# Decoder layer on one core: cross attention with the values as the stationary operand, weights normalised ahead of their transposes, and no transposes of the output

## The reference

```python
q = (query @ Wq.T).reshape(batch, seq, 16, 64)     # 16 heads of 64
k = (key   @ Wk.T).reshape(batch, seq, 16, 64)
v = (value @ Wv.T).reshape(batch, seq, 16, 64)
weights = jnp.einsum('bqhd,bkhd->bhqk', q, k) * scale + reweight + causal
weights = jax.nn.softmax(weights, axis=-1)
out = jnp.einsum('bhqk,bkhd->bqhd', weights, v).reshape(batch, seq, -1)
return out @ Wo.T + bo
```

## Time and profile before

| | |
|---|---|
| median of 3 runs | 1305.52 us (1304.98 to 1308.28) |
| the profiled execution | 1298.92 us, of it span 1297.2 us |
| PE busy | 1187.7 us, 92% |
| PEld busy | 988.4 us, 76% |
| DVE busy | 830.5 us, 64% |
| ACT busy | 648.9 us, 50% |
| POOL busy | 153.4 us, 12% |
| mean granted clock of TensorE | 0.944 |

### The profile page before, as it was taken

How to read it: one execution, slowest core, us unless ns; L and a number is a source line. 1 busy time by engine, 2 the same in 40 slices (tenths; PEclk the granted TensorE clock), 3 DMA queues, 4 the chain that set the end, 5 groups by cost and what they waited for, 6 DMA issues and landing times.

```text
span 1297.2 us, 22848 instructions
## 1 busy us (share of the span) xinstructions
PE 1187.7 (92%) x8404; PEld 988.4 (76%) x8404; DVE 830.5 (64%) x2630; ACT 648.9 (50%) x1363; POOL 153.4 (12%) x184
## 2 busy tenths in 40 slices
PE   3899899889889989979999988989999999999996
PEld 3767788766788877769876778877778787788875
DVE  5725437873646874645776445778778677788563
ACT  2236533235634224744233643438666776968663
POOL 4899302200000000000000000000000000000000
PEclk9999979999979999998999987989998899999898
DMA  8200000100000010000010200120000010000000
GB/s 313 85 17 1 1 1 1 49 17 1 2 1 1 1 53 14 2 1 1 1 34 17 68 1 1 41 82 25 1 1 25 1 33 25 1 18 26 26 17 17
DMA packets 21388, 33.27 MB, mean 26 GB/s; under 512 B 11424, under 2 KB 12192, under 8 KB 20128
## 3 DMA queue, kind: packets, MB, share of 16 engines
q1 hardware_dynamic: 21280, 31.82, 7.3%
HBM read 27.62 MB, written 4.19 MB: 25 GB/s over the span
## 4 chain that ended last, share of the span: by engine, by line
PE 74%; DVE 13%; ACT 8%; issue 3%; POOL 1%; DVEq 0%; ACTq 0%; POOLq 0%
PE ps L504 41%; PE ps L747 6%; PE ps L645 4%; PE ps L663 2%; PE ps L662 2%; DVE z L1589 2%; DVE arena L1779 2%; PE ps L661 2%; DVE arena L1406 2%; PE ps L637 1%; PE ps L635 1%; PE ps L608 1%; ACT L1263 1%; PE ps L621 1%; PE ps L886 1%
## 5 line engine op out<-in xcount | busy, mean ns | idle before, releaser
L504 PE MATMUL ps<-arena,wts 128*128 128x256 f16 (+1 forms) x1344 | 189.2, 295 | 20.6 <-ACTq L477 20.6
L504 PE MATMUL ps<-wts,arena 128*128 128x256 f32 (+2 forms) x1008 | 201.0, 357 | 3.8 <-ACT arena L1347 3.2
L504 PEld LDWEIGHTS ps<-arena,wts 128*128 128x128 f16 (+1 forms) x1344 | 153.2, 115 | 49.1 <-issue 20.5
L504 PEld LDWEIGHTS ps<-wts,arena 128*128 128x128 f32 (+1 forms) x1008 | 154.6, 155 | 41.3 <-ACT arena L1347 4.0
L1589 DVE SCALAR_TENSOR_TENSOR z<-ps,small,z 128x256 f32<-128x256 f32 x256 | 123.9, 484 | 41.3 <-PE ps L747 26.8
L1197 ACT ACTIVATE pq<-ps 128x512 f32<-128x512 f32 x72 | 43.0, 598 | 169.1 <-PE ps L504 169.0
L747 PE MATMUL ps<-wts,pq 128*128 128x256 f32 x512 | 120.8, 380 | 6.2 <-DVE z L1589 6.2
L747 PEld LDWEIGHTS ps<-wts,pq 128*128 128x128 f32 x512 | 92.6, 190 | 18.7 <-DVE z L1589 4.9
L645 PE MATMUL ps<-ident,pq 128*128 128x128 f32 x384 | 73.9, 306 | 33.1 <-DVE arena L1506 12.3
L1106 ACT ACTIVATE pq<-pq,nms 128x128 f32<-128x128 f32 x128 | 50.9, 398 | 92.1 <-DVE nms L1479 92.1
L1477 DVE CUSTOM_DVE_ANT_0 pq<-ps,mb 128x128 f32<-128x128 f32 x128 | 36.6, 286 | 86.0 <-PE ps L637 85.7
(11 more groups left out here) (286 smaller groups left out, 2402.3 us busy)
## 6 DMA issues: line engine op xcount, KB each, us to landing
cT<-in_cT SPq DMA_DIRECT2D x16, 256.0 KB, 2.7
wts<-in_up SPq DMA_DIRECT2D x1, 2304.0 KB, 15.5
wts<-in_down SPq DMA_DIRECT2D x1, 2304.0 KB, 20.5
xT<-in_xT SPq DMA_DIRECT2D x8, 256.0 KB, 4.0
xin<-in_x SPq DMA_DIRECT2D x8, 256.0 KB, 2.9
xmid<-xin SPq DMA_DIRECT2D x8, 256.0 KB, 2.0
wts<-in_w SPq DMA_DIRECT2D x2, 1024.0 KB, 5.0
wts<-in_c SPq DMA_DIRECT2D x16, 128.0 KB, 3.2
```

The lines of the kernel that those rows point to most:

```text
L504: ins = mm(out_, l, r, start=(n == 0), stop=(n == len(pairs) - 1))
```

## The change

- **Values.** The stationary operand is now the 64 value channels of a head (`V[:, ... AD]`, the column of ones isn't used), and the transposed weights stream: 256 columns for the first half of the keys, 128 for the second. Both heads of a pair go in one iteration (odd `n`), to partitions 0 to 63 and 64 to 127. The output then has channels on partitions, as the output projection wants it; four heads fill a bank (`("OT", s, m)`).
- **Sums.** They are taken by the exps themselves (`accum_out` to `rsum(n)`). DVE takes the reciprocals (`attn_sums`, head n-1).
- **Division.** GpSimd multiplies the weights by them, in place, in front of the transposes (`attn_norm`, mark `Pn`). It does so for every head of every turn; in turn 0 between the expert chunks and those for K, V and Q.
- **Gone:** `turn_out` with its 32 transposes per turn, and DVE's division by sums.
- **Offsets.** Transposes of head n-4 in place of n-3, values of heads n-7 and n-6 in place of n-5, copies out (`turned`, `turned_low`) of head n-7 for both sequences inside the loop. Output projection of sequence 0 in iteration 24 (was 26), of sequence 1 with the first pair of experts (was with the second), transposes of z2 in iteration 28 (was 29).
- **Scratch.** `half` lies at the end of `arena[1]` and no longer on `z2[1]`. The wait for `halfq` and `halfo` above stays as it was.

```diff
+        def rsum(n):
+            return small[1][:, 128 + 2 * (n % 8):130 + 2 * (n % 8)]
...
-        half = flat(z2[1][:, :, :]).bitcast(F16).rearrange("p (i n e) -> p i n e", i=2, n=4)
+        half = arena[1][:, 11 * KC * T:12 * KC * T].bitcast(F16).rearrange("p (i n e) -> p i n e", i=2, n=4)
...
             def attn_turn(n, s, h):
 
-                eng.wait_ge(*pe.at("E", s, h))
+                eng.wait_ge(*pe.at("Pn", s, h))
...
             def attn_values(n, s, h):
 
+
+                if h % 2 == 0:
+                    return
                 V = carve_a(s)[0][2]
-                eng.wait_ge(*pe.at("PT", s, h, "out"))
                 eng.wait_ge(*pe.at("V", s, "out"))
...
-                mm(o[:, c0:c0 + AD + 1], pt[:, 0:P], v0, start=True, stop=True)
-                mm(o[:, c1:c1 + AD + 1], pt[:, P:T], v0, start=True, stop=False)
-                ins = mm(o[:, c1:c1 + AD + 1], pt[:, T:SBLK], v1, start=False, stop=True)
+                m = h // 2
+                if m % 2 == 0:
+                    take(("OT", s, m), ("OT", s, m, "out"), 6 + (n // 4) % 2)
+                o, c = ps[:, 6 + (n // 4) % 2, :], (m % 2) * T
+                for j in range(2):
+                    eng.wait_ge(*pe.at("PT", s, h - 1 + j, "out"))
+                for j in range(2):
+                    hj, row, pt = h - 1 + j, slice(AD * j, AD * j + AD), ptbuf(n - 1 + j)
+                    v0 = V[:, hj * (AD + 1):hj * (AD + 1) + AD]
+                    v1 = V[:, (AH + hj) * (AD + 1):(AH + hj) * (AD + 1) + AD]
+                    mm(o[row, c:c + T], v0, pt[:, 0:T], start=True, stop=False)
+                    ins = mm(o[row, c + P:c + T], v1, pt[:, T:SBLK], start=False, stop=True)
...
-                for n in range(len(UNITS) + 5):
+                for n in range(len(UNITS) + 6):
                     if n < len(UNITS) and n % 2 == 0:
                         attn_scores(n, UNITS[n][0], UNITS[n][1] // 2)
-                    if 0 <= n - 3 < len(UNITS):
-                        attn_turn(n - 3, *UNITS[n - 3])
-                    if 0 <= n - 5 < len(UNITS):
-                        attn_values(n - 5, *UNITS[n - 5])
-
-                    if OUT0 <= n < OUT0 + AM // 2:
-                        turn_out(0, 2 * (n - OUT0), 4 + n % 2)
-                    if n == OUT0 + AM // 2:
+                    if 0 <= n - 4 < len(UNITS):
+                        attn_turn(n - 4, *UNITS[n - 4])
+                    if 0 <= n - 6 < len(UNITS):
+                        attn_values(n - 6, *UNITS[n - 6])
+
+                    if n == OUT0 + 2:
                         out_proj(0, 4 + n % 2)
-                    if n == OUT0 + 7:
+                    if n == OUT0 + 6:
                         transposes(0, "zT2", z2[0], ("z2", 0), 4 + n % 2)
...
-                A(pb[:, 0:P], pb[:, 0:P], ACT.Exp, scale=-1.0, bias=nm[:, 0:1]).then_inc(*act.up())
-                A(pb[:, P:SBLK], pb[:, P:SBLK], ACT.Exp, scale=-1.0, bias=nm[:, 1:2]).then_inc(
+                rs = rsum(n)
+                A(pb[:, 0:P], pb[:, 0:P], ACT.Exp, scale=-1.0, bias=nm[:, 0:1], accum_out=rs[:, 0:1]).then_inc(*act.up())
+                A(pb[:, P:SBLK], pb[:, P:SBLK], ACT.Exp, scale=-1.0, bias=nm[:, 1:2], accum_out=rs[:, 1:2]).then_inc(
                     *act.up(("E", s, h)))
...
+            def attn_sums(n, s, h):
+                eng.wait_ge(*v.at("E", s, h))
+                V_.reciprocal(rsum(n), rsum(n)).then_inc(*v.up(("R", s, h)))
...
                     if n < len(UNITS):
                         attn_max(n, *UNITS[n])
-                    if 0 <= n - 3 < len(UNITS):
-                        attn_pt(n - 3, *UNITS[n - 3])
-                    if 0 <= n - 6 < len(UNITS):
-                        attn_norm(n - 6, *UNITS[n - 6])
...
+                    if 0 <= n - 1 < len(UNITS):
+                        attn_sums(n - 1, *UNITS[n - 1])
+                    if 0 <= n - 4 < len(UNITS):
+                        attn_pt(n - 4, *UNITS[n - 4])
+                    if 0 <= n - 7 < len(UNITS):
+                        turned_low(n - 7, *UNITS[n - 7])
+                    if n == OUT0 + 3:
                         residual(0, "xo", z[0][:, :, :], z2[0], "ln_2")
...
+            def attn_norm():
+                for n, (s, h) in enumerate(UNITS):
+                    pb, rs = pbuf(n), rsum(n)
+                    eng.wait_ge(*po.at("R", s, h))
+                    G.tensor_scalar(pb[:, 0:P], pb[:, 0:P], rs[:, 0:1], None, ALU.mult).then_inc(*po.up())
+                    G.tensor_scalar(pb[:, P:SBLK], pb[:, P:SBLK], rs[:, 1:2], None, ALU.mult).then_inc(
+                        *po.up(("Pn", s, h)))
+
             po.stage("halves")
...
+                if mark == "halfk":
+                    po.turn = 0
+                    attn_norm()
+                    po.turn = None
                 if read:
...
+            po.stage("norms")
+            for g in range(1, TURNS):
+                po.turn = g
+                attn_norm()
+            po.turn = None
```

More of the change, by code:

```diff
@@ L817, in _ @@
                             if e == 0:
-                                for m in range(0, AM, 2):
-                                    turn_out(1, m)
-                            if e == 2:
                                 out_proj(1)
@@ L1199, in _ @@
                         if s == 0:
-                            if e == 0:
-                                for m in range(0, AM, 2):
-                                    turned(1, m)
                             if e == 4:
@@ L1507, in lower, with turned_low @@
                                  parts[:, 0].rearrange("p k t -> p (k t)"), ALU.subtract).then_inc(*v.up(outmark))
-            def turned_low(s, m):
-                if v.turn:
+            def turned_low(n, s, h):
+                m = h // 2 - 1
+                if v.turn and h % 4 == 3:
                     lower(("OT", s, m), ("OTh", s, m), oth(s, m), ("OT", s, m, "out"))
@@ L1670, in _ @@
                     for e in range(0, NE, 2):
-                        if e == 0 and s == 0:
-                            for m in range(0, AM, 2):
-                                turned_low(1, m)
                         if e == 0:
```

70 lines of the change are left out of this document (21 added, 49 removed).

## The result

The changed kernel takes **1336.8 us** (median of 4 runs, 1336.1 to 1343.49) against 1305.25 (4 runs): ratio 1.026, 95% interval 1.0209 to 1.031. It is slower by 2.6%; forecast was 1296, a little faster, and 1336.8 lies beyond the upper end of the range. The profiled execution took 1337.22 us at a span of 1335.5.

What follows compares the result with a forecast made beforehand. TensorE, with waits at the out-transposes, was taken to bound the attention loop, then GpSimd. Loops -35.1, expert-stage start -6.0 and turn 0 +32.0 summed to -9.1 on 1305.52, so 1296 us; range 1263 to 1326.

Steps and rivals of the forecast that it cites:

- The loop as a whole: Attention loop, first score to last values: 2.7 + 49.6 + 6 + 2.2 = 60.5 us; three turns give -35.1.
- The chain of the earlier trace is gone: Attention loop's end: the waits around the out-transposes, four iterations taking 13.2 us, were said to vanish.
- The loop passes from TensorE to GpSimd: Steady attention loop: GpSimd at 1.55 us per head becomes the bound, above TensorE's 1.27; no faster than today's 1.45.
- GpSimd's price: Two multiplications per head in the attention loop: 1.55 us by the trace's rows, bounds 1.13 and about 1.8.
- Score pairs 3.1 us apart: Sign expected in the profile of the attention loop: successive score pairs start 3.1 us apart.
- GpSimd dry for 6 us in the epilogue: Sequence 0's epilogue: GpSimd idles 3.9 us at the output projection and 1.8 at z2's transposes, together about 6.
- Start 2.7, end 2.2: Attention loop: 2.7 us before GpSimd's first multiplication, 2.2 after its last for transposes, copy and values.
- Readout of the sums, 0.15 each: ScalarE's exps in the attention loop: also giving sums costs about 0.15 us each, making 1.4 a head.
- Start of the expert stage, -6.0: Behind the loops of turns 1 to 3: 16 out-transposes of sequence 1, 2.06 us, go each time, -6.0 in all.
- Turn 0, +32.0: Turn 0's expert stage: the residual waits for GpSimd's late K, V, Q chunks, next turn at 275.7 against 243.65.
- the slower loop: Rival, attention loop: readouts of 0.3 us or a GpSimd head of 1.75 give +16, 1322 us; chance 0.18.
- The clock rival: Rival inside the attention loop: TensorE's clock falls to 1.2 GHz, 2.3 us a head, +96, near 1392; chance 0.05.

Runs made afterwards that it cites:

- e2: The changed kernel with VectorE's low halves of the copied output two heads later: 1308.65 us.
- e4: The changed kernel without the division by the sums, so no multiplications on GpSimd: 1290.89 us.
- e6: e5 with the division by the sums left out as well: 1262.63 us.
- e5: The changed kernel with both edits, no wait for `halfq` in turn 0 and low halves two heads later: 1273.09 us.
- e9: e5 with ScalarE's copies of the transposed weights put ahead of its exps: 1264.31 us.
- e10: e9 with VectorE instead of GpSimd dividing every fourth head: 1243.26 us.
- e1: The changed kernel without the residual's wait for `halfq` in turn 0: 1305.35 us.
- e8: e5 with only the output projection of sequence 0 in the other one of banks 4 and 5: 1265.39 us.
- e12: e10 with the output projection of sequence 0 in the other one of banks 4 and 5: 1249.92 us.

## Why the prediction was wrong

- **The step that failed** is in "The loop as a whole": "The chain of the earlier trace rows is gone". It isn't. The transposes of the output are gone, but the hand-over from ScalarE's copy to VectorE's low halves now stands inside the loop, eight times a turn. ScalarE makes the copy at the end of an iteration and VectorE wants it in the same iteration, ahead of the next maximum. The prediction's paragraph on VectorE doesn't list `turned_low` and goes by busy time ("isn't near a bound"), and the sum holds no term for the wait. Price: 12 to 13 us in each of turns 1 to 3 (e2), 28 us in the medians, and the same with no division at all (e4 against e6). About a quarter of it falls where the holes are, the rest behind the output projection, in part at a lower granted clock. No run has left the low halves in place and moved ScalarE's copy forward instead.
- **"The loop passes from TensorE to GpSimd"**: the size was right (1.49 us a head for 1.55), the role wrong. e4 takes GpSimd out and the loop stays at 73.7. Only with the stall gone do pairs settle at GpSimd's 2.97, in some turns of e2 and e5 and in most of e9, and even there the whole loop is as long without GpSimd (e6), since another place in a queue, ScalarE's copy behind its exps, holds the pair at 2.83 on average. e10, with that copy first and less work on GpSimd, has 2.67.
- **GpSimd's price**: the row-based 1.55 was right. By the Trainium skill, page "GPSIMD Engine Reference", section 3.1, it would have been about 0.6 (an estimate by that page); the measured 602 and 923 ns decide.
- **Score pairs 3.1 us apart**: 3.19 and 3.54 in turns 1 to 3; 2.83 on average in turn 0. Right by number in part, from another cause.
- **GpSimd dry for 6 us in the epilogue**: it was 7.89 + 3.45 and five smaller holes behind them, 16.2 in all. The two places and their cause (projection, z2) were right. With the stall gone three holes are left in turn 1 of e2 (5.30, 0.86, 2.99), 9.15 in all: still half as much again as the 6, since I had counted from the last head's end and not the recovery behind it.
- **Start 2.7, end 2.2**: 2.97 (352.69 - 349.72) and 4.5 (419.8 to 424.3, at a granted clock of 0.72).
- **Readout of the sums, 0.15 each**: the rows list 189 ns each, but in the timeline exp, exp and copy start 0.38 and 0.49 apart (363.92, 364.30, 364.79) where it was 0.30 and 0.40, so 0.09 each. Harmless.
- **TensorE's pair at 2.5**: right, 2.47; the four-call value form takes 0.80 (365.86 to 366.66) where 0.85 was read off.
- **Start of the expert stage, -6.0**: the stretches behind the loops of turns 1 to 3 fell by 3.1, 3.8 and 2.2, so 9.1 in all.
- **Turn 0, +32.0**: the residual ran at 222.0 instead of 217.2 and the next turn began at 278.5 instead of 275.7, +34.9 against 243.65. Right in cause, place and nearly in size; e1 confirms it with 31.5 in the medians.
- **The rivals**: the slower loop (0.18) came, but through neither of its two prices. The clock rival came in part, but not in its place. In the steady stretch the granted clock is 1.00, in the changed kernel and also where GpSimd is the bound (turn 2 of e2, 558 to 583: GpSimd busy for all 25.00 us, clock 1.00). Behind the output projection it is 0.82, and 1.00 there once the stall is gone (e2), worth 5.1 us of TensorE's time in turn 1.

The sum closes with what was measured: -9.1, +45.4 for loops of 74.6, 76.3 and 76.0 instead of 60.5, +2.9 for turn 0, -3.1 behind the loops, +2.3 for the rwkv part of turn 1 make +38.4; the span grew by 38.3. Of the 45.4, e2 gives back 37.5; the other 7.9 are what its loops still take over 60.5.

## What to carry to other kernels

- When work moves into a loop of in-order queues, cost each piece twice: by its time, and by the latest thing it waits for with what stands behind it. Eight instructions of 0.69 us in a queue that was half idle cost 12 us a loop; two iterations later they cost next to nothing.
- A buffer that moves takes its waits with it. The wait for `halfq` protected nothing any more and cost 31 us (e1).
- Ask "which is the floor" by leaving the suspect out. GpSimd at 1.49 us a head, next to a pace of 1.68 (3.19 and 3.54 a pair), looked like the floor and wasn't.

## What the runs showed of the hardware

**VectorE blocked by GpSimd.** In e1 GpSimd's chunks run beside the experts of turn 0. Its timeline (POOL and DVE):

```profile
200.37 1.16 POOL L2082 TENSOR_TENSOR arena<-wts,arena 128x512 f16<-128x512 f32 x1
200.41 1.16 DVE L1538 TENSOR_TENSOR small<-small 128x32 f32<-128x32 f32 x1
...
203.69 0.19 DVE L1553 SCALAR_TENSOR_TENSOR small<-small 128x32 f32<-128x32 f32 x1
```

A 32-column operation of VectorE with both inputs in SBUF takes 1158 ns beside a GpSimd instruction that began just before it, and as long as that one, where its like take 190. The same instruction takes 1144 ns in e5, and 192 in the changed kernel and 191 in e4, where no chunk runs beside it. The mixing of the next turn (L1399, 16 times) takes 808 ns on average against 682 in the same stretch of before, while the gated sums, which read PSUM, stay at 484 in both. The Trainium skill, page "SBUF — State Buffer", section "Who interferes with whom", says as a rule that a VectorE instruction with two SBUF inputs contends with a GpSimd instruction that reads SBUF, and that what they contend for is an exclusive lock; this trace agrees, with 1158 ns beside one of 1160. VectorE's maximum (L1470), which reads PSUM, shows none of it in the attention loop: its median is 291 ns with GpSimd's multiplications (changed kernel) and without them (e4). The blocking is part of the 4.8 us that e1 keeps on the way to turn 1: 16 x 0.126 = 2.0 in the mixing, 1.0 at L1538; in e4 and e6, with GpSimd's chunks over early, that way takes 138.7. The rest of the 4.8 isn't placed.

**The last part and the clock.** The matmuls behind the last attention loop are the same in all the changed kernels, but took 492.5 us (e8, e12) to 505.9 us (e2, e5) in the profiled runs, at mean granted clocks of 0.946 to 0.914. The runs of the kernel before spread from 1292.3 to 1310.8 us, with a granted clock of 0.950 in the first and 0.932 in the last; only one of them was profiled, so where they differ isn't shown. A difference between two single runs is no evidence below that spread of 18 us, which is why loops were compared in the traces and not only totals. What decides it stays open.
